# Expert loops in steps of two pairs of tiles, weights addressed as bytes, each half finished by itself

## What is computed

```python
logits = xf @ Wr + br                       # 8064 tokens, 64 experts
topk_logits, topk_idx = jax.lax.top_k(logits, 2)
gates = jax.nn.softmax(topk_logits, axis=1)
for e in range(E):
    h = jax.nn.relu(xf @ W1[e] + b1[e])     # 64 -> 128
    y = h @ W2[e] + b2[e]                   # 128 -> 64
    out = out + combine[:, e:e + 1] * y
```

## Time and profile before

| | |
|---|---|
| median of 3 runs | 884.67 us |
| the profiled execution | 888.75 us |
| its span, first to last instruction | 886.8 us |
| mean granted PE clock | 0.741 |
| PE, DVE, ACT, POOL busy | 57%, 73%, 38%, 62% |
| expert loop in the span | 615 to 797 us |

### The profile page before, as it was taken

One profiled execution on the slowest core, in us unless ns is written; L12 is line 12 of the kernel. 1 busy time (PEld: TensorE's weight loads), 2 busy tenths in 40 slices (PEclk: granted clock), 3 DMA queues, 4 the chain that ended last, 5 costly groups with the idle time before them and its releaser, 6 DMA issues.

```text
span 886.8 us, 8725 instructions
## 1 busy us (share of the span) xinstructions
PE 501.2 (57%) x2132; PEld 320.0 (36%) x2132; DVE 645.4 (73%) x1160; ACT 339.2 (38%) x597; POOL 551.6 (62%) x398
## 2 busy tenths in 40 slices
PE   4916903365666665575556920002999999980340
PEld 3815801121211121121116910001777777760240
DVE  1379548999999989999974999991444444459951
ACT  2311384555555455454527710000444444430110
POOL 1002204699999999999940007777777167757774
PEclk9965655677787787878785555555999999995565
DMA  6999900000000000000000000302899899961131
GB/s 229 366 136 108 30 0 0 0 0 0 1 0 0 0 0 0 0 0 0 0 0 1 1 0 27 89 25 62 229 262 265 230 256 263 269 192 26 25 99 37
DMA packets 100734, 71.63 MB, mean 81 GB/s; under 512 B 29330, under 2 KB 87314, under 8 KB 100690
## 3 DMA queue, kind: packets, MB, share of 16 engines
q1 hardware_dynamic: 73154, 54.39, 28.0%
q0 software_dynamic: 8064, 8.27, 3.5%
q10 hardware_dynamic: 19472, 8.47, 3.3%
HBM read 48.12 MB, written 29.29 MB: 87 GB/s over the span
## 4 chain that ended last, share of the span: by engine, by line
POOL 35%; PE 22%; DVE 15%; issue 15%; SPq 4%; DMA 4%; ACT 3%; POOLq 1%; DVEq 0%; ACTq 0%
POOL hh_ring L419 13%; PE ps L611 8%; POOL w_ring L404 8%; POOL sorted_rows L438 7%; POOL xt L446 7%; PE ps L600 4%; DMA x_w<-packed 3%; PE ps L470 3%; SPq L328 2%; PE ps L538 2%; DVE mi L1072 1%; PE ps L521 1%; PE ps L593 1%; DVE hh_ring L1004 1%; DVE w_ring L1060 1%
## 5 line engine op out<-in xcount | busy, mean ns | idle before, releaser
L538 PE MATMUL ps<-hh_ring,ident 128*128 128x512 f32 x272 | 181.7, 807 | 153.1 <-POOL hh_ring L419 116.4
L438 POOL DMA_INDIRECT sorted_rows<-xp,slot_i x126 | 122.1, 969 | 115.0 <-DVE slot_i L1098 76.9
L404 POOL TENSOR_TENSOR w_ring<-xt,bc 128x1024 f32<-128x1024 f32 x64 | 153.8, 2405 | 37.3 <-DVE xt L973 37.3
L446 POOL DMA_INDIRECT xt<-expert_out,slot_i x126 | 120.7, 958 | 65.6 <-issue 37.8
L419 POOL TENSOR_TENSOR hh_ring<-hh_ring,bc 128x1024 f32<-128x1024 f32 x63 | 148.4, 2356 | 17.9 <-DVE hh_ring L1004 14.6
L538 PEld LDWEIGHTS ps<-hh_ring,ident 128*128 128x128 f32 x272 | 58.2, 234 | 275.8 <-POOL hh_ring L419 184.7
L1004 DVE TENSOR_TENSOR_SCAN hh_ring<-ps,w_ring 128x1024 f32<-128x1024 f32 x64 | 145.9, 2280 | 0.1
L611 PE MATMUL ps<-x_w 128*128 128x192 f32 x504 | 117.0, 355 | 0.0
L744 ACT ACTIVATE ps<-dt_t,a_exp 128x1024 f32<-128x1024 f32 x64 | 71.5, 1118 | 79.9 <-DVE w_ring L982 79.9
L748 ACT ACTIVATE ps<-dt_t,a_exp 128x1024 f32<-128x1024 f32 x64 | 71.5, 1118 | 65.1 <-DVE hh_ring L1004 65.1
L1172 DVE COPY x_w<-ps 128x128 f32<-128x128 f32 x126 | 36.8, 292 | 72.0 <-PE ps L611 69.0
(11 more groups left out here) (174 smaller groups left out, 707.9 us busy)
## 6 DMA issues: line engine op xcount, KB each, us to landing
x_w<-packed SPq DMA_DIRECT2D x252, 96.5 KB
sorted_rows<-pad_rows SPq DMA_DIRECT2D x2, 4096.0 KB, 18.0
x_w<-sorted_rows SPq DMA_DIRECT2D x32, 256.0 KB
expert_out<-x_w ACTq DMA_DIRECT2D x126, 64.0 KB
packed<-in_L_ffn_W SPq DMA_DIRECT2D x3, 2048.0 KB, 36.2
x_w<-in_x SPq DMA_DIRECT2D x7, 448.0 KB, 10.1
sorted_rows<-xp,slot_i POOLq DMA_INDIRECT x126, 2.1
xt<-expert_out,slot_i POOLq DMA_INDIRECT x126, 2.4
```

Of the source, the lines that this page charges most:

```text
L404: pool.tensor_tensor(w_ring[:, k % 4, :].rearrange("p (d s) -> p d s", s=S), up3[:, bass.ds(c * DC, DC), :], bc[:, k:k + 1, :].broadcast_t ...
L438: pool.indirect_dma_start(out=sorted_rows[k], out_offset=bass.IndirectOffsetOnAxis(ap=slot_i[:, k, l:l + 1], axis=0), in_=xp1[:, l, 0:C], ...
L446: pool.indirect_dma_start(out=y[:, l, :], out_offset=None, in_=expert_out[k], in_offset=bass.IndirectOffsetOnAxis(ap=slot_i[:, k, l:l + 1] ...
L538: ins = pe.matmul(ps[:, i, :], ident[:, :], hh_ring[:, buf, i * BANK:(i + 1) * BANK], start=(k < 0), stop=(k == N - 1), skip_group_check=True)
```

## The change

Work is done in steps of up to two pairs: 32 steps for each half (`STEPS`), the last of one pair. In each step PE does both transposes, then four hidden matmuls, then four output matmuls; ACT copies both transposed tiles with one instruction and stores both pairs with one DMA; DVE copies both pairs' outputs with one instruction; relus stay one for each tile. PSUM banks for rows and hidden layer alternate between steps, but banks 6 and 7 now both belong to one step, so outputs(i) waits for y_copy(i-1). The weight ring has 8 slots, and a slot becomes free with the step that used it. `te` is multiplied by the bytes of an expert's block, and the weight DMAs address `packed` as bytes. PE, ACT and DVE run a loop of their own for each half; SyncE's loop still runs over all pairs.

```diff
-WRING = 7
+WRING = 8
+STEPS = -(-PAIRS // 2)
+BLOCK = 4 * P * WROW
+def pairs_of(i):
+    h, d = divmod(i, STEPS)
+    return range(h * PAIRS + 2 * d, h * PAIRS + min(2 * d + 2, PAIRS))
+def step_of(n):
+    return n // PAIRS * STEPS + n % PAIRS // 2
...
+            blocks = packed.rearrange("e p n -> (e p n)").bitcast(U8)
             def load_weights(h, q, es):
                 n = h * PAIRS + q
                 if n >= WRING:
-                    sp.wait_ge(s_yb, n - WRING + 1)
+                    sp.wait_ge(s_yb, step_of(n - WRING) + 1)
                 for t in range(2):
-                    sp.dma_start(w_in[:, n % WRING, t, :], packed[bass.ds(es[t], 1), :, :].rearrange("a p n -> (a p) n")
+                    sp.dma_start(w_in[:, n % WRING, t, :].bitcast(U8),
+                                 blocks[bass.ds(es[t], BLOCK)].rearrange("(p n) -> p n", p=P)
                                  ).then_inc(s_win[n % WRING], 16)
...
-                    sp.wait_ge(s_rT, g * PAIRS + min(UNIT * (v + 1), PAIRS))
+                    sp.wait_ge(s_rT, g * STEPS + UNIT // 2 * (v + 1))
...
+            def rows_T(i):
+                for j, n in enumerate(pairs_of(i)):
+                    u = unit_of(n)
+                    if n % PAIRS % UNIT == 0:
+                        pe.wait_ge(s_rows[u % RING], 16 * (u // RING + 1))
+                    last = pe.transpose(ps[:, i % 2, j * P:(j + 1) * P], rows_in[:, u % RING, n % PAIRS % UNIT, :],
+                                        ident[:, :])
+                last.then_inc(s_rT, 1)
+            def hidden(i):
+                for n in pairs_of(i):
+                    pe.wait_ge(s_win[n % WRING], 32 * (n // WRING + 1))
+                pe.wait_ge(s_rTc, i + 1)
+                for j, n in enumerate(pairs_of(i)):
+                    for t in range(2):
+                        last = pe.matmul(ps[:, 2 + 2 * (i % 2) + t, j * P:(j + 1) * P],
+                                         w_in[t * C:(t + 1) * C, n % WRING, t, 0:HID],
+                                         xT_e[t * C:(t + 1) * C, i % 2, j, :], start=True, stop=True)
                 last.then_inc(s_hid, 1)
+            def outputs(i):
+                pe.wait_ge(s_reluA, i + 1)
+                pe.wait_ge(s_reluB, i + 1)
+                if i >= 1:
+                    pe.wait_ge(s_yb, i)
+                for j, n in enumerate(pairs_of(i)):
+                    for t in range(2):
+                        last = pe.matmul(ps[:, 6 + j, t * OUT:(t + 1) * OUT], hT_e[:, i % 2, t, j, :],
+                                         w_in[:, n % WRING, t, 0:OUT], start=True, stop=True)
                 last.then_inc(s_yps, 1)
+            for h in range(2):
+                o, z = h * STEPS, (h + 1) * STEPS
+                rows_T(o)
+                rows_T(o + 1)
+                hidden(o)
+                for i in range(o, z):
+                    if i + 2 < z:
+                        rows_T(i + 2)
+                    if i + 1 < z:
+                        hidden(i + 1)
+                    outputs(i)
...
+            def store(i):
+                q, m = pairs_of(i)[0] % PAIRS, len(pairs_of(i))
+                act.wait_ge(s_yb, i + 1)
+                rows = expert_out[i // STEPS].rearrange("(u p t) d -> u p t d", p=P, t=2 * UNIT)
+                act.dma_start(rows[q // UNIT, :, 2 * (q % UNIT):2 * (q % UNIT) + 2 * m, :],
+                              y_e[:, i % YRING, 0:m].rearrange("p q t d -> p (q t) d")).then_inc(s_st[i % YRING], 16)
+            for h in range(2):
+                o, z = h * STEPS, (h + 1) * STEPS
+                xT_copy(o)
+                xT_copy(o + 1)
+                relu_A(o)
+                for i in range(o, z):
+                    if i + 2 < z:
+                        xT_copy(i + 2)
+                    if i + 1 < z:
+                        relu_A(i + 1)
+                    if i > o:
+                        store(i - 1)
+                store(z - 1)
...
-                dve.tensor_scalar(te[:, k * P:(k + 1) * P], ps[0:1, 2, 0:P], float(E - 1), None, ALU.min
+                dve.tensor_scalar(te[:, k * P:(k + 1) * P], ps[0:1, 2, 0:P], float(E - 1), float(BLOCK), ALU.min, ALU.mult
...
+            def y_copy(i):
+                m = len(pairs_of(i))
+                if i >= YRING:
+                    dve.wait_ge(s_st[i % YRING], 16 * (i // YRING))
+                dve.wait_ge(s_yps, i + 1)
+                dve.tensor_copy(y_e[:, i % YRING, 0:m],
+                                ps[:, 6:6 + m, 0:2 * OUT].rearrange("p q (t d) -> p q t d", d=OUT)[:, :, :, OUT - C:OUT]
                                 ).then_inc(s_yb, 1)
+            for h in range(2):
+                o, z = h * STEPS, (h + 1) * STEPS
+                relu_B(o)
+                for i in range(o, z):
+                    if i + 1 < z:
+                        relu_B(i + 1)
+                    y_copy(i)
```

More of the change, by code:

```diff
@@ L8 @@
 U32 = mybir.dt.uint32
+U8 = mybir.dt.uint8
 ALU = mybir.AluOpType
@@ L274, in experts @@
             return nc.values_load_multi_w_load_instructions(te[0:1, bass.ds(g, IDS)], engines=[engine],
-                                                            min_val=0, max_val=E - 1, skip_runtime_bounds_check_because=
-                                                            "te is a count of experts, clamped to E - 1")[1]
+                                                            min_val=0, max_val=(E - 1) * BLOCK,
+                                                            skip_runtime_bounds_check_because="te is a count of experts, "
+                                                            "clamped to E - 1, times the bytes of a block")[1]
         block = ctx.enter_context(nc.Block())
@@ L443, in _ @@
                 for j in range(YRING):
[L444 removed]
+                    pool.wait_ge(s_st[j], 16 * (((k + 1) * STEPS + YRING - 1 - j) // YRING))
                 for l in range(L):
@@ L585, in _ @@
             pe.wait_ge(s_tei, 2)
[L588 to L601, removed]
-                last.then_inc(s_hid, 1)
@@ L604, in outputs @@
[L604 to L612, removed]
-                last.then_inc(s_yps, 1)
-            rows_T(0)
-            rows_T(1)
@@ L626, in _ @@
+            for h in range(2):
[9 more added lines that the diff above has]
+                    outputs(i)
             pe.wait_ge(s_b2, 32)
-            pe.wait_ge(s_yb, 2 * PAIRS)
+            pe.wait_ge(s_yb, 2 * STEPS)
@@ L822, in store @@
-            def store(n):
-                h, q = n // PAIRS, n % PAIRS
-                act.wait_ge(s_yb, n + 1)
-                rows = expert_out[h].rearrange("(u p t) d -> u p t d", p=P, t=2 * UNIT)
-                act.dma_start(rows[q // UNIT, :, 2 * (q % UNIT):2 * (q % UNIT) + 2, :],
-                              y_e[:, n % YRING]).then_inc(s_st[n % YRING], 16)
-            xT_copy(0)
-            xT_copy(1)
-            relu_A(0)
-            for n in range(2 * PAIRS):
-                if n + 2 < 2 * PAIRS:
-                    xT_copy(n + 2)
-                if n + 1 < 2 * PAIRS:
-                    relu_A(n + 1)
-                if n > 0:
-                    store(n - 1)
@@ L840, in _, with xT_copy, relu_A @@
-            store(2 * PAIRS - 1)
+            def xT_copy(i):
+                m = len(pairs_of(i))
+                act.wait_ge(s_rT, i + 1)
+                act.activation(xT_e[:, i % 2, 0:m, :].rearrange("p q n -> p (q n)"), ps[:, i % 2, 0:m * P], ACT.Copy
+                               ).then_inc(s_rTc, 1)
+            def relu_A(i):
+                act.wait_ge(s_hid, i + 1)
+                if i >= 2:
+                    act.wait_ge(s_yps, i - 1)
+                for j, n in enumerate(pairs_of(i)):
+                    last = act.activation(hT_e[:, i % 2, 0, j, :], ps[:, 2 + 2 * (i % 2), j * P:(j + 1) * P], ACT.Relu,
+                                          bias=w_in[:, n % WRING, 0, HID + C:WROW])
+                last.then_inc(s_reluA, 1)
```

40 lines of the change are left out of this document (11 added, 29 removed).

## The result

The changed kernel takes 892.24 us (median of 20 runs, 884.49 to 897.82) against 886.24 us for the kernel before (20 runs): a ratio of 1.0063, 95% interval 1.0044 to 1.0082. The ratio leaves out one slow run of the changed kernel (897.82), which the median of 20 includes. It is slower by 0.6%. The forecast was 880, with 868 to 891: the time lies above the range, and near the 890 to 894 that rival (B), the shorter ring, gave. The profiled execution took 894.74 us, its span 892.6.

The account below looks back on a forecast made before the run. PE, with SyncE close, bounded the old loop; the ring would bound the new: 158.1 + 2.8 + 3.9 + 5.1 + 3.3 + 2.0 = 175.2 us, 5.4 less. The median 884.67 became 879.3, rounded to 880 (868 to 891).

Parts of the forecast that it names:

- rival (B): The shorter weight ring makes the kernel slower: landings of 4.0 to 4.2 us give 890 to 894 us; chance 0.20.
- ring formula: Weight ring of four steps: the step period is (4.16 + landing)/3, taken as 2.55 us, bounds 2.36 and 3.3.
- PE's saving: PE changes into and out of 64-row weights once per two-pair step: 2.36 us instead of 2.76, 25 us less.
- The copy on PE's path: outputs(i) waits for DVE's doubled copy, taken as 0.44 us; hidden behind PE's other work by 0.2 us.
- The boundary: Between the halves PE, ACT and DVE drain: 2.0 us more, bounds 0 and 4.
- SyncE's slot: Time per weight issue on SyncE: one register instruction goes, 0.515 to 0.436 us; eight issues in 3.4 us.
- rival (C): The byte view leaves SyncE's time per weight issue unchanged: period 2.63 us, 884.3 us, no change; chance 0.23.
- The landing: Weights land 3.5 us after a step's last issue; landings above 4 us in the chain would mean rival (B).
- The rarer delays: SyncE's table reads (5.1 us) and long issues (3.3 us) reach PE, partly covered by 0.57 us idle per step.
- short steps, start and end: Loop time outside full steps: 2.8 us for two one-pair steps, 3.9 us for start and end.
- The clock: PE's clock falling in the new waits would make the forecast wrong; half speed doubles 0.98 us per pair.
- The other signs: SyncE's waits for DVE's copy grow, PE's weight waits from 7.8 to 15 us or more, GpSimd's idle near 4.

Follow-up runs that it names:

- both edits: The changed kernel with ten weight slots and one double-size DMA per pair (second tile's own expert left out): 869.17 against 886.68 us for the kernel before, 0.9810.
- e12: The changed kernel, unedited, run again on an ordinary chip: 890.35 against 886.68 us for the kernel before, 1.0029.
- e8: The changed kernel with one double-size weight DMA per pair (second tile's own expert left out): 876.67 against 885.80 us for the kernel before, 0.9896.
- e13: The changed kernel with ten weight slots instead of eight and three output buffers instead of four, ordinary chip: 875.89 us, 0.9883 of the kernel before.
- all three edits: The changed kernel with ten weight slots, slots freed after PE's outputs, and one loop over both halves: 876.59 us, 0.9892 of the kernel before, ordinary chip.

## Why the prediction was wrong

Two terms of the sum were too small, both of SyncE: the slot of an issue (0.436 us, measured 0.474) and, the larger part, the delays that SyncE's other work brings into the ring (8.4 us, measured some 14). The ring formula was right, and so was the landing time in it. The result lies near rival (B), but not for that rival's reason.

The loops side by side, each from its own profile, from the landing of the first rows to the last store. The changed kernel's two profiles differ by 3.5 us, so the others are no surer than that:

| kernel | loop, us | what it waits for |
|---|---|---|
| before | 180.6 | PE busy |
| after | 184.4 (again: 187.9) | ring and SyncE |
| after, slot freed earlier | 179.5 | ring and SyncE |
| after, ten slots | 171.5 | SyncE |
| after, one issue for a pair | 171.0 | ring |
| after, both | 164.5, of it some 5 for late rows | almost nothing in the halves |

In the kernel with both edits PE is busy for 35.00 and 34.82 of 35 us. The forecast was 175.2 us for the loop; 184.4 is 9.2 more. Of the other 3 us between 880 and 892.24, 1.6 lie in the kernel before, whose median of 20 runs (886.24) is above the 884.67 that the forecast started from, and 1.57 lie before the loop (below).

**PE's saving: right.** Steps are 2.37 us apart without a weight wait (2.36 forecast), and the kernel with both edits runs so throughout. The Trainium skill ("TensorEngine Tiling (Array Packing)", Key Properties) says that a change of tiling mode drains the engine; the trace fits that, with 11.8/63 = 0.19 us of idle time on the way into the 64-row weights, but it can't tell a drain from a weight load that isn't loaded ahead.

**The copy on PE's path: right.** The double copy takes 0.421 us (0.44 forecast), and the outputs matmuls waited for it four times, 1.9 us in all. Two of them, 0.25 and 0.68 us, are at the end of the first half, where PE has nothing else left to do:

```profile
L1204 DVE COPY x_w<-ps 128x256 f32<-128x256 f32 x64 | 26.9, 421 | 64.9 <-PE ps L634 64.9
L634 PE MATMUL ps<-x_w 128*128 128x192 f32 x504 | 101.4, 344 | 1.9 <-DVE x_w L1204 1.9
```

**The boundary: right as a row.** From the outputs of the last full step but one of half 0 to the first of half 1 it takes 714.27 - 705.33 = 8.94 us, where two full steps and a short one without a wait take 2 x 2.37 + 1.38 = 6.12. That is 2.8 more, where 2.0 was forecast (bounds 0 and 4).

```profile
705.33 1.52 PE ps L634 x8
...
709.73 0.90 PE ps L634 x4
...
714.27 1.50 PE ps L634 x8
```

**SyncE's slot: wrong, the first step that failed, and the smaller one.** FUSED_REGOPS went, as assumed, but the issue got longer. SyncE's weights' line after (ns min/median/max) and one undisturbed run of eight:

```profile
L343 SPq MOVE x_w<-packed x252: 29/29/38, 556.8 to 792.1; - x126
L343 SPq DMA_DIRECT2D x_w<-packed x252: 332/381/2243, 556.9 to 792.1; - x126
```
```profile
651.29 3.70 SPq L343 DMA_DIRECT2D x_w<-packed  x8
```

The issue takes 381 ns, not 333; the slot is (3.70 - 0.38)/7 = 0.474 us, not 0.436. Half of the expected 0.079 came. Eight issues take 3.70, between the forecast's 3.4 and the 3.95 of rival (C). Three slots in a round make 3 x 0.038/3 x 62 = 2.4 us of the miss.

**The landing: right, though the chain makes it look wrong.** L was taken as 3.5 us, counted from the last of a step's four issues. The trace of the changed kernel gives it for every step, as the time from that issue to the last semaphore update of the four DMAs (a few updates in a hundred are missing): over the 60 steps that wait for a slot it is 3.58 in the median and 3.53 in the mean, from 2.27 to 5.81. The landings of 3.93 to 6.10 in the chain after are no measure of it. The chain picks out long ones, and it counts from an earlier issue. Nor were the four of the earlier trace rows all that the chain before had; it has six, with these two:

```profile
727.27 3.23 DMA x_w<-packed
...
736.84 4.94 DMA x_w<-packed
```

Their mean is 4.29, but over the 119 pairs that waited for a slot the trace of before has 3.44. The argument that a chain picks out the long ones was sound; that 3.5 was so close is in part luck, since it rested on two rows. With L at 4.3 and the other parts as they are without a delay, the formula would give 2.87 us, more than the 2.83 measured with all delays in it. The sign that was to tell rival (B), landings above 4 in the chain, thus pointed to it for the wrong reason: its time came, its longer landings didn't.

**The rarer delays: wrong, the step that decided.** The forecast gave table reads and long issues 5.1 + 3.3 = 8.4 us, in the belief that SyncE sits idle for 0.57 us of a step and hides the rest. The whole round, in the terms of the forecast, as means over the steps that wait for a slot (us; from issue times, semaphore updates, the ends of DVE's copies and the starts of the hidden matmuls in each trace):

| part of the round | forecast | after | after again (e12) | one issue (e8) | ten slots (e13) |
|---|---|---|---|---|---|
| computing and copy, beyond one step | 2.75 | 2.76 | 2.78 | 2.74 | 2.73 |
| slot free until SyncE's first issue | 0.10 | 0.48 | 0.46 | 0.15 | 1.69 |
| first to last issue | 1.31 | 1.46 | 1.49 | 0.48 | 1.49 |
| last issue until all have landed | 3.50 | 3.53 | 3.56 | 4.07 | 3.82 |
| landed until PE starts on them | 0 | 0.34 | 0.44 | 0.47 | 0.81 |
| sum | 7.66 | 8.57 | 8.73 | 7.91 | 10.54 |
| divided by steps in the ring less one | 2.55 | 2.86 | 2.91 | 2.64 | 2.64 |

Without a delay the second and the last part are 0.03 and 0.09 and the third 1.42, so the formula with L at 3.5 gives (2.76 + 0.03 + 1.42 + 3.5 + 0.09)/3 = 2.60, close to the forecast's 2.55. The mean step was (184.4 - 2.8 - 3.9 - 2.0)/62 = 2.83, with the forecast's terms for short steps, start and end, and boundary. The difference of 0.23 is 14 us in 62 steps, where 8.4 were forecast: some 6 us of the miss; the slot and the 0.09 before PE starts are most of the rest.

Most of the delays are SyncE's. A round was longer by 0.45 + 0.04 + 0.25 = 0.74 us than one without a delay: 0.45 before SyncE's first issue, 0.04 between its issues, and 0.25 in which the weights lay ready and PE hadn't come. In 20 of the 60 steps its first issue came more than 0.3 us after the slot was free. A table read made not one step late but two or three in a row: after the one at 633.96 the steps were 1.62 and 1.42 late, after the one at 658.73 1.09, 1.07 and 0.71. With the real slot SyncE's work is 4 x 0.474 + 0.24 for the rows + 2.08/8 = 0.26 for the table (2083 ns, every eighth step) = 2.40 us of a step, so there is little room to catch up in. In the other 40 steps SyncE was ready within that time and the round trip of the ring set the pace. That is why neither is the bound alone: a late step holds PE up, an early landing gives nothing back (in 17 of the 60 steps PE came to the weights more than 0.3 us after they had landed). Relieving either one took some 13 us off the loop and both 20 (25 without the late rows). The columns show it too: with one issue SyncE is hardly late and the ring is left; with ten slots the ring has time to spare, and what is left is SyncE, late by 1.69. Long issues were fewer than counted with, six of over 0.6 us (0.65 to 2.24) against ten, so the count was not what failed. How the 14 us divide between table reads, long issues and the scatter of landings was not tested by a run of its own.

On the rule of the Trainium skill quoted for rival (B) ("DMA: Bandwidth & Descriptors", Latency and other measured facts) the trace agrees in kind: the weights of the four steps issued before the loop, at 182 GB/s, had landed 2.47 to 2.77 us after their last issue, those of the loop after 3.58 in the median. But the burst of four issues didn't make landings longer than they had been: 3.44 in the mean before, 3.53 after.

**The clock: a small part.** It was named as what could go wrong, and it did once in this profile. In the chain above, the steps at 653.95 and 656.80 take 2.43 for 1.50 and 1.12 for 0.72, 1.3 us more, after a wait of 1.64; the granted clock from 652 to 660 is 0.79 on average, between the levels of 1.2 and 2.4 GHz. A longer wait, the 1.93 us before 733.57, was followed by no such fall (1.00 from 731 to 738), so the length of one wait doesn't tell. The second profile of the changed kernel has two such places, at 687 and 711, with 0.72 and 0.77. All engines in the first window:

```profile
652.00:660.00 8.00, 6.77 (x42) 5.87 (x44) 2.07 (x6) 1.95 (x6) 5.93 (x7) 0.79 0.94 264
```

**The other signs: as written.** SyncE's waits for DVE's copy grew from 11.1 to 34.6, PE's for weights more than the 15 us named. GpSimd's slack grew instead of falling to 4, because the second half's loop got longer. The end of the span followed the loop's end: the last store is 800.81 - 795.42 = 5.4 us later and the span 892.6 - 886.8 = 5.8 longer. Of the 5.4, 1.57 lie before the first rows, in work that the change doesn't touch; 3.8 are the loop's.

```profile
SPq L343 <- DVE x_w L1204: 34.6, 33, 9.0
```

## What to carry to other kernels

When work is batched, count a ring of buffers in units of what frees them at once: eight slots freed two at a time are four, and the period is at least (compute + copy + issues + landing) / (units - 1). Don't read the landing time from the chain of work that ended last, which picks out the long ones: in the kernel before its mean was 4.29 us, where all transfers that waited for a slot had 3.44. Work out how much of the new period the queue that feeds the ring is busy: where little is left (2.40 of 2.6 us here), a delay of the queue holds up several steps in a row, and neither ring nor queue hides the other's delays. Enlarge the ring in the same change.

## What the runs showed of the hardware

- A weight DMA addressed in bytes, with source and destination viewed as bytes, takes SyncE 381 ns to issue, the one in float32 333 ns (252 issues in each kernel; the median was 381 or 382 in all six profiles from ordinary chips that have it). Whether the view or the form of the address does it wasn't separated. The register work saved is 0.037 us and a gap.
- Weights of a step, 4 DMAs of 96.5 KB in packets of 772 bytes: 3.58 us in the median from the last issue to the last landing, at some 250 GB/s of all traffic; 2.5 to 2.8 at 182 GB/s. As two DMAs of 193 KB: 4.07 us in the mean at 273 to 280 GB/s, 4.40 at 302 to 306.
- Single issues of SyncE take up to 2.24 us in the changed kernel, and up to 2.81 with all three edits, where the median is 0.38. Why wasn't settled.
- On two chips the same kernels are 190 us longer, with stalls of ACT and DVE of up to 28 us at a time and of PE of up to 42 in the expert loop. Why wasn't settled.
